# Conditioned two-layer transformer on one core: the identity transposed into the idle MLP bank in TensorE's holes

## The reference

```python
# layer 0
ada = silu(cond) @ ada_w.T + ada_b             # six vectors of 256 per sequence: g1 g2 s1 s2 sh1 sh2
h = ln(x) * (1 + s1) + sh1
x = x + (attention_with_rope(h) @ proj_w.T + proj_b) * g1      # 16 heads of 16
h2 = ln(x) * (1 + s2) + sh2
x = x + (gelu(h2 @ fc1_w.T + fc1_b) @ fc2_w.T + fc2_b) * g2    # 1024 hidden
# layer 1
tp = swiglu(cond @ w_t1 + b_t1) @ w_t2 + b_t2  # shift1 scale1 shift2 scale2
h = rmsnorm(x, g1) * (1 + scale1) + shift1
x = x + attention_with_rope(h) @ w_ao + b_ao
h = rmsnorm(x, g2) * (1 + scale2) + shift2
x = x + swiglu(h @ w_fc + b_fc) @ w_fo + b_fo
```

## Time and profile before

| | |
|---|---|
| median of 3 runs | 794.48 us (793.76 to 796.32) |
| the profiled execution, its own time | 798.87 us |
| its span in the profile | 797.0 us |
| mean granted TensorE clock | 0.983 |
| PE busy | 753.3 us (95%) |
| DVE busy | 627.0 us (79%) |
| ACT busy | 478.3 us (60%) |
| POOL busy | 291.4 us (37%) |

### The profile page before, as it was taken

One profiled execution on the slowest core, in us unless ns is written; L12 is line 12 of the kernel. 1 busy time (PEld: TensorE's weight loads), 2 busy tenths in 40 slices (PEclk: granted clock), 3 DMA queues, 4 the chain that ended last, 5 costly groups with the idle time before them and its releaser, 6 DMA issues.

```text
span 797.0 us, 13586 instructions
## 1 busy us (share of the span) xinstructions
PE 753.3 (95%) x4800; PEld 467.1 (59%) x4800; DVE 627.0 (79%) x1097; ACT 478.3 (60%) x761; POOL 291.4 (37%) x267
## 2 busy tenths in 40 slices
PE   5979999999999999999999999999999999999697
PEld 3643334466545754565546664667646684668397
DVE  3878997798878988888788899968868878865454
ACT  1217764687658765786658876665466655565332
POOL 0502114443354535452464336232343232422343
PEclk9969999999999999999999999999999999999899
DMA  8569570433142411351141433541133411100000
GB/s 320 157 178 297 137 213 14 146 116 73 40 137 90 108 41 40 107 146 42 40 133 54 146 94 112 168 99 32 44 113 114 107 41 49 21 1 1 28 1 27
DMA packets 34163, 76.22 MB, mean 96 GB/s; under 512 B 4528, under 2 KB 9264, under 8 KB 33840
## 3 DMA queue, kind: packets, MB, share of 16 engines
q1 hardware_dynamic: 34096, 75.35, 33.3%
HBM read 39.42 MB, written 35.65 MB: 94 GB/s over the span
## 4 chain that ended last, share of the span: by engine, by line
PE 75%; DVE 7%; DMA 6%; issue 4%; POOL 3%; ACT 3%; SPq 2%; ACTq 0%; DVEq 0%; POOLq 0%
PE ring L1037 18%; PE ps_o L967 13%; PE ps_b L1054 12%; PE ring L937 9%; PE ring L952 8%; PE ring L901 5%; DVE top L1233 3%; PE ring L1007 3%; DMA kt<-scratch 3%; PE ring L914 2%; POOL sines L1603 2%; PE ring L978 2%; ACT pr L1489 1%; PE ring L883 1%; DMA qt<-top_t 1%
## 5 line engine op out<-in xcount | busy, mean ns | idle before, releaser
L1233 DVE TENSOR_REDUCE top<-ring 128x2 f32<-128x1024 f32 x256 | 307.4, 1221 | 53.5 <-PE ring L952 51.2
L1489 ACT ACTIVATE pr<-ring 128x1024 f32<-128x1024 f32 x256 | 255.9, 1024 | 84.0 <-PE ring L937 77.2
L1646 POOL TENSOR_TENSOR act_l<-mlp,act_h 128x256 fp32r<-128x256 f32 x128 | 102.8, 803 | 240.1 <-DVE act_h L1315 240.1
L967 PE MATMUL ps_o<-pr,va 128*17 128x512 f32 x1024 | 133.2, 602 | 0.1
L952 PE MATMUL ring<-kt,qt 48*128 48x512 f32 x512 | 112.9, 458 | 10.0 <-DMA kt<-scratch 4.5
L937 PE MATMUL ring<-qt,kt 49*128 49x512 f32 x512 | 114.1, 466 | 6.3 <-DMA qt<-top_t 3.2
L1526 ACT ACTIVATE mlp<-ring,col 128x256 f32<-128x256 f32 x128 | 60.5, 473 | 83.9 <-PE ring L1037 70.2
L937 PEld LDWEIGHTS ring<-qt,kt 49*128 49x128 f32 x512 | 46.5, 184 | 86.9 <-issue 41.8
L1037 PE MATMUL ring<-hh,wl 128*128 128x256 f32 x384 | 84.1, 301 | 2.9 <-DVE hh L1290 0.9
L1301 DVE SCALAR_TENSOR_TENSOR mlp<-mlp 128x256 f32<-128x256 f32 x128 | 59.3, 463 | 34.1 <-ACT mlp L1533 23.8
L952 PEld LDWEIGHTS ring<-kt,qt 48*128 48x128 f32 x512 | 48.5, 189 | 63.0 <-issue 22.4
(11 more groups left out here) (89 smaller groups left out, 1025.1 us busy)
## 6 DMA issues: line engine op xcount, KB each, us to landing
scratch<-high SPq DMA_DIRECT2D x48, 512.0 KB, 5.1
qt<-scratch SPq DMA_DIRECT2D x64, 192.0 KB, 3.7
kt<-scratch SPq DMA_DIRECT2D x64, 192.0 KB, 4.6
scratch<-low SPq DMA_DIRECT2D x16, 512.0 KB, 5.6
mlp<-in_w_split SPq DMA_DIRECT2D x20, 256.0 KB, 3.3
xs<-in_x SPq DMA_DIRECT2D x4, 512.0 KB, 5.6
out_x<-xs SPq DMA_DIRECT2D x3, 512.0 KB, 2.9
pr<-in_w_ada SPq DMA_DIRECT2D x2, 512.0 KB, 7.6
```

The costliest lines, as they stand in the source:

```text
L967: last = nc.tensor.matmul(ps_o[32 * h:32 * h + HD + 1, :], va[:, u % 2, t, QUAD * g + h, :], pr[:, slot, :], start=(t == 0), stop=(t == T ...
L1233: nc.vector.tensor_reduce(top[:, n % 2, 0:4 * T].rearrange("p (e c) -> p e c", e=2)[:, :, c], pair[:, :, :], AX_X, ALU.max, negate=True).t ...
L1489: nc.scalar.activation(pr[:, at % NP:at % NP + 2, :], pair[:, :, :], ACT.Exp, scale=SCALE).then_inc(free, 1)
L1646: nc.gpsimd.tensor_tensor(act_l[:, at % 2, :], src, act_h[:, at % 2, :].bitcast(F32), ALU.subtract).then_inc(act_l_in, 1)
```

## The change

A helper `spare(count)` is added to TensorE's program. It transposes the identity into the first 128 columns of `ps_b`, `count` times; nobody reads what it writes, and it signals nothing. It is called

- 24 times in unit 0's first `norm_turn`, ahead of its wait for the normed x, and 7 times behind its turns;
- 40 times in the last unit's `norm_turn(LAST, 1)`, ahead of its wait for the normed x and behind a wait for `b_free` (the bank has been read for unit 6), and 16 times behind its turns;
- 2 times behind each of the eight parts of `net_2`;
- 2 times behind each of the first three column groups of `mod_0(1)`.

For every norm turn the wait for `xn_in` now stands behind these.

```diff
+                def spare(count):
+                    for _ in range(count):
+                        nc.tensor.transpose(ps_b[:, 0:P], eye[:, :], eye[:, :])
                 def norm_turn(u, n):
                     name = TURNED[n]
-                    pe.wait_ge(xn_in, norm_at(u, n) + 1)
                     if u == 0 and n == 0:
                         pe.wait_ge(s_small[2], 16)
+                        spare(24)
+                    if u == LAST and n == 1:
+                        pe.wait_ge(b_free, u * HALVES)
+                        spare(40)
+                    pe.wait_ge(xn_in, norm_at(u, n) + 1)
...
                         last.then_inc(full, 1)
+                    if u == 0 and n == 0:
+                        spare(7)
+                    if u == LAST and n == 1:
+                        spare(16)
...  net_2, in the loop over n
+                        if n % share == 0:
+                            spare(2)
...  mod_0, in the loop over n
+                        if m == 1 and n < 2 * KC - 1:
+                            spare(2)
```

## The result

| | before | after |
|---|---|---|
| median | 793.79 us (14 runs, 792.14 to 797.33) | 799.25 us (14 runs, 794.45 to 804.51) |
| ratio | | 1.0073, 95% interval 1.0052 to 1.0093 |
| span of the profiled execution | 797.0 us | 797.9 us |

The forecast was 796.0 us, slower by 0.19%, in a range up to 799.2. The change costs some 5.5 us, three to four times what the sum gave, and lands just above the range.

What follows compares the result with a forecast made beforehand. TensorE, busy 95%, was taken as the bound, so spares pay only where it is idle or slow-clocked. Terms +1.9, 0, +0.4 and -0.8 sum to +1.5 us on 794.48, giving 796.0 us; 8-in-10 range 792.8 to 799.2.

Steps and rivals of the forecast that it cites:

- the sum: Whole program: the terms +1.9, 0, +0.4 and -0.8 added, +1.5 us.
- Part 2: Six spares in `mod_0(1)`, 12 in the first six parts of `net_2`: hidden in TensorE's holes before first peaks, 0 us.
- Part 3: Four spares in the last two parts of `net_2`, on the chain between second and third peaks: +0.4 us.
- Part 1: Unit 0's first turn: 24 spares ahead cost 5.1 us, earlier full clock returns 2.8 and 0.4: +1.9 us.
- Part 4: Last unit's turn: 40 spares make it 1.1 us late, held clock saves 1.9 on 48 up products: -0.8 us.
- Rival A: Everywhere: spares don't raise or hold the clock; +7.6 us, 802.1 us; chance 0.08.
- Rival B: Start delays all, low clock lasts through unit 1's four L901, beyond 59 us; +3.6 us, 798.1 us; chance 0.22.
- Rival C: Clock stays up through 44 to 57 us, start cheap, end gains fully; -3.3 us, 791.2 us; chance 0.08.

Runs made afterwards that it cites:

- small_early: Kernel before plus only the spares in `mod_0(1)` and the first six parts of `net_2`, none in its last two: ratio 1.0011, mean 796.24 us.
- after_again: The changed kernel itself, unaltered, timed and profiled a second time: ratio 1.0047 against before, mean 798.81 us.

## Why the prediction was wrong

**The step that failed: Parts 2 and 3, the spares between the small products.** Forecast +0.4, measured +2.9 ± 0.5. Part 2 put 18 of them at nothing, because holes of TensorE cover 2.0 us. The cover wasn't there. In after the first peaks followed a spare with no wait, 1.1 us later than their data allowed. Two things in that step were wrong. The hole of 2.38 us is an execution's, not the kernel's: others have 0.7 to 2.0. And the cover was looked for on TensorE alone, while a piece that is late there is late for everyone who waits for it. The six spares in `mod_0(1)` delay the second pair's q and k by 0.5 us (2.32 us from the start of `mod_0(1)` to it, 1.81 before), and with them rope and DVE's queue behind it. POOL's subtraction is timed by a DMA and doesn't move, so the 0.23 us between DVE's last small copy and it (starts at 37.64 and 37.87 in the profile of before) was gone. DVE lost 2 us, the last gate came 1.2 to 1.8 us later against v, and with it the peaks and the first maximum.

Of the other term, Part 3, +0.4 looks too small as well: the last four cost 1.3 ± 0.3 of rest. But no trace shows where. Together with the 0.5 of small_early that makes 1.8 us, beside the 2.1 of the fit; the 0.8 us through more low clock has no place shown either.

**Part 1** was mis-sized: +1.9 forecast, +2.9 ± 0.4 measured. v starts at 20.7 on average in the six profiles with the 24 and at 19.2 in the eleven without any at the start, 1.5 us later. The mechanism is that of the forecast: no hole, 4.0 to 5.2 us of spares, paid back in part by a full clock for the L901. What comes on top of the 1.5 isn't located.

The profiles say roughly where both early groups together lose. In the four with both, the first top turn (quad 0) is at 55.3 us on average, in the six with neither at 53.5, 1.8 earlier. For quad 4 it is 118.3 against 115.8, for quad 5 138.8 against 132.3 (three of the four have the fall at 122 us, none of the six), for the last `project` 747.0 against 742.1. So the time is lost by quad 5, and nothing more is added behind it.

**Part 4** was right in each term: the clock held, the turn 1.07 us late (1.1 forecast), 48 up products 1.87 us faster (1.9). From the start of `project` to the end of the span the nine profiles without the last unit's spares take 51.2 to 52.4 us (51.5 on average). Seven of the eight with 40 and 16 take 50.6. The eighth, after_again, takes 52.3, with a fall just ahead of the hole (747.1 to 750.5 us), which the spares come too late for. Over many runs the part is worth -1.5 ± 0.4, which doesn't contradict -0.8.

**Whether a transpose counts.** The forecast took it that it does, against the Trainium skill ("TensorE: Matmul & The Clock Gate", Part 4: PE-mode transpose). The runs bear that out: in after the clock was up at 13.5 us, when TensorE had done nothing but 4-column products and identity transposes, and 40 + 16 spares held it through the last hole. The Trainium skill's statement differs from these measurements, and they decide. Rival A is out.

**Rival B** came nearest in size (+3.6), by a way that the traces show only in small part. The first low stretch of after ended at 57.9 us, not beyond 59, and was shorter (10.2 us) than before; unit 1's four L914 took 2.65 us against 2.09, 0.6 more where B had 1.2. **Rival C** didn't come.

**The base.** I summed from one execution whose own time was 5 us over the median, with falls at 142 and 360 us that are chance. That changed no term, but the scatter of the low clock (17 to 37 us from run to run in before, worth up to 9 us between single runs) deserved a wider range.

## What to carry to other kernels

Work that only keeps an engine busy is free only in a hole of its own engine that nothing in order behind it must pass, and whose consumers have slack too. Measure the hole in more than one execution, and look for the slack on each engine that waits for what is moved, down to small operations next to another engine's long one. A warm-up pays ahead of the first real work, not in front of a piece that is already released. Where the clock falls at places that change with the execution, size a change over many runs, and by the low clock's time in each run beside the total.

## What the runs showed of the hardware that I had not expected

A DVE copy or scalar operation of 128x8 elements takes 0.17 us alone, and a copy of 128x128 takes 0.21. In nine profiles one of them took 2.0 to 2.4 us when it started inside a POOL operation of 2.35 us over 128x1024; it ended 0.03 to 0.08 us behind it. Not every operation is held: the norm statistics (L1146 before) lie inside the same POOL operation in before and take 0.41 to 0.43 us as elsewhere, and in small_early an addition that reads PSUM (`small<-ring,col`, 128x16) started inside it at 36.31 and took 0.16. The Trainium skill ("SBUF — State Buffer", Terms: shared port pair) says that DVE and GpSimd take one pair of ports in turn for a whole instruction and that the loser is fully blocked. The trace agrees for the copies and scalar operations, with the ends that coincide.

The granted clock explains most of a kernel's scatter: 0.48 us of time for each us of low clock within one kernel, over all the sets of runs, and three quarters of the variance.

The clock was still low at the end of sixteen 4-column products, 3.4 us on end (7.0 to 10.5 us), in all 17 profiles in which they came first. With 24 transposes of the identity behind them the clock rose at 13.2 to 15.8 us (six profiles), with 20 ahead of them at 8.1 to 10.4 (three), without any at 16.5 to 19.6 (eleven).
